# First scores of an attention and expert kernel spread over four PSUM banks, and the first k's parts built right behind the first q's

## The chip, the cores and the metric

One Trainium2 chip, one NeuronCore. The metric is the device time of one execution in microseconds (us). Engines: PE (TensorE, matmuls), DVE (VectorE), ACT (ScalarE), POOL (GpSimd), SP (SyncE, which here issues DMAs only). ACT and POOL have DMA queues of their own beside SP's.

## The reference, cut to what matters

```python
def attention(x_norm, encodings, ...):            # 16 sequences, each 128 channels x 512 tokens
    qkv = transpose(x_norm) @ w_in.T + b_in       # 8 heads of 16
    scores = einsum("bqhd,bkhd->bhqk", q, k) / 4
    scores = where(abs(q_index - k_index) <= 64, scores, lowest)
    o = softmax(scores) @ v
    y = relu(transpose(o @ w_out.T + b_out)) * encodings
    return einsum("nit,io->not", y, w_ct) + b_ct

x = x + attention(layernorm(x), ctx)
x = x + experts(layernorm(x))                     # 16 experts, top 2, and one shared expert
```

## The kernel before, in words

The work falls into three stages: the attention of 16 sequences, a drain that mixes the last sequences with the first blocks of the shared expert, and the experts. Only the very beginning of the first stage is touched by the change.

**Order of the work.** Each engine runs a list written out by hand. A global counter, the unit `U`, runs from -26 upward, and each engine's `step(U)` calls what is due. `at(U, k)` gives sequence n when `U = 8 n + k`; `piece(U, k)` gives sequence n and one of its eight pieces j when `U = 8 n + j + k`. A piece is one block of 128 queries and four of the eight heads. Engines execute their lists strictly in order and meet through semaphores. So what stands behind a waiting call on an engine waits too.

**The first q and k (n = 0).** The layer norm of a sequence is `first_moments` on DVE (L1177, L1179; due at -26), three small operations on POOL, and `normalise1` on ACT (L932; due at -21, but for sequence 1 at `SECOND_NORM`, -10). `first_moments(n)` waits for `normalise1(n-1)`. Then PE projects q (`project_q`, L630, at -13) and k (`project_k`, L638, at -9; for n = 0 directly behind). A float32 value is carried as three bfloat16 parts. For q: `first_q` (ACT L947, -12), `residue_q` (DVE L1189, -12), `second_q` (ACT L951, -11), `third_part` (POOL L439, -11). For k: `first_k` (ACT L957, -8), `residue_k` (DVE L1195, -8), `second_k` (ACT L961, -7), `third_part` (POOL, -7). The parts are copied by DMA into stacks of 96 rows, `qstack` and `kstack`, six DMAs each (groups 0 to 5; `Q_PARTS` and `K_PARTS` say which part a group holds). SP issues them with `send_q` (L316) and `send_k` (L321); two of the first k's (groups 1 and 4) are issued by ACT (L1014). Behind these on ACT stand `biases_out`, `normalise1(2)` (at -5) and `first_q(1)` (at -4), on DVE `residue_q(1)` (-4) and `first_moments(3)` (-2).

**Scores.** `scores(n, j, half)` (PE L583, due at -1) multiplies the stacks, two heads of a piece into the bank `s1[half]`, each 192 or 256 columns. `maximum(n, j, half)` (DVE L1208, due at -1) adds the mask and takes the row maxima of that bank and counts the semaphore `rowmax` up. There are two banks `s1`, so the scores of unit u + 1 in a bank wait for the maxima of unit u in it. Between the scores PE also does `project_k` of the next sequence (at -9), `project_v` (L644, at 1), `project_q` (at -13) and `turn_max` (L654, at 8).

**Second scores.** When the 16 halves of a sequence have their maxima, POOL splits the maxima into three parts (`split_max`, L456 to L462, at 7), PE transposes them (`turn_max`, which also waits for `residue_k` of sequence n + 2), DVE copies them out (`max_rows`, L1216, at 9), SP sends them into the q stack (L347, at 9), and from unit 11 on PE computes the scores again, shifted by the maxima, into the two banks `s2` (`shifted_scores`, L601). ACT takes their exponentials (L974), POOL cuts the band (L468, L470), PE multiplies with v (L618). From there on each unit carries a piece of each of these steps. The banks `s2` are empty until unit 11.

Quoted, the wait that paces the first scores:

```python
after(pe, rowmax, 2 * UNITS * n + 2 * j + half - 1)
```

Of the kernel before, what the change touches and what calls it, by code (L numbers as in the profile page):

```python
# [28 lines left out]
ALU = mybir.AluOpType  # L29
# [5 lines left out]
HEADS, D = 8, 16  # L35
# [12 lines left out]
UNITS = 2 * QB  # L48
RING = 4
WD_RING = 3  # L50
FIRST_UNIT, LAST_UNIT = -26, UNITS * (SEQS - 1) + 40
DRAIN, DRAINED, SOON = UNITS * (SEQS - 1) + 20, 8, 2
FIRST_SOON = DRAIN - 11
SECOND_NORM = -10
MASKED = -1e38

# [49 lines left out]
def xattn_moe_kernel(nc, x, ctx_in, const_f, const_b, w_small, w_gu, w_d, sw_gu, sw_d, out):  # L107
    es = ExitStack()
    with es:
# [116 lines left out]
        bank = [es.enter_context(nc.psum_tensor(f"bank{i}", [P, 512], F32)) for i in range(8)]  # L226
        s1, s2, oacc, misc = bank[0:2], bank[2:4], bank[4:6], bank[6:8]

        consts_in, bands_in, weights_in, shared_in = (  # L230
            sem(s) for s in ("consts_in", "bands_in", "weights_in", "shared_in"))
# [70 lines left out]
        def _(sp):  # L302
# [33 lines left out]
            def step(U):  # L336
# [19 lines left out]
                    store_turned(n)  # L356
                if (n := at(U, -10)) is not None:
                    send_q(n, (1, 3))
                if (n := at(U, -9)) is not None:
                    sp.wait_ge(q_p2, n + 1)  # L360
                    send_q(n, (2, 4))
                if (n := at(U, -7)) is not None:
                    sp.wait_ge(q_p3, n + 1)
                    send_q(n, (5,))
                    sp.wait_ge(k_p1, n + 1)
                    send_k(n, (0,))
                if (n := at(U, 25)) is not None:
                    after(sp, gated_ready, n - 1)
                    sp.dma_start(enc[n % 2], ctx_in[n]).then_inc(enc_in[n % 2], 16)
                if (n := at(U, -6)) is not None:  # L370
                    send_k(n, (2, 5))
                    if n > 0:
                        sp.wait_ge(k_p2, n + 1)
                        send_k(n, (1,))
                if (n := at(U, -5)) is not None:
# [45 lines left out]
        def _(pool):  # L421
# [57 lines left out]
            def step(U):  # L479
                if (n := at(U, -24)) is not None:  # L480
                    inverse_deviation(0, n, mom1, eps1, rstd1)
                    mean_shift(0, n, rstd1, shift1)
                if (n := at(U, 30)) is not None:
                    gate(n)
                if (n := at(U, 7)) is not None:
                    split_max(n)
                if (n := at(U, 23)) is not None:
                    split_reciprocals(n)
                if (n := at(U, 35)) is not None:
                    inverse_deviation(1, n, mom2, eps2, rstd2)  # L490
                    mean_shift(1, n, rstd2, shift2)
                if p := piece(U, 11):
                    cut_band(*p)
                if (n := at(U, -11)) is not None:
                    third_part(n, qres, qparts, q_p2, q_p3)
                if (n := at(U, -7)) is not None:
                    third_part(n, kres, kparts, k_p2, k_p3)

            v.memset(kstack[0][STACK:STACK + 3, :, :], -1.0).then_inc(ones_set, 1)
# [57 lines left out]
        def _(pe):  # L557
# [15 lines left out]
            def scores(n, j, half):  # L573

                blk, hg = j // 2, j % 2
                lo, w, _ = window(blk)
                if j == 0 and half == 0:
                    pe.wait_ge(q_in[n % RING], STACK_DMAS * (n // RING + 1))
                    pe.wait_ge(k_in[n % RING], STACK_DMAS * (n // RING + 1))
                after(pe, rowmax, 2 * UNITS * n + 2 * j + half - 1)  # L580
                for i in range(2):
                    h = 4 * hg + 2 * half + i
                    last = mm(s1[half][:, 256 * i:256 * i + w],  # L583
                              qstack[n % RING][0:STACK, h, P * blk:P * blk + P],
                              kstack[n % RING][0:STACK, h, lo:lo + w], start=True, stop=True)
                last.then_inc(s1_ready, 1)

            def shifted_scores(n, j, half):
# [3 lines left out]
                if j == 0 and half == 0:  # L592
# [3 lines left out]
                        pe.wait_ge(ones_in, 16 * (RING - 1))  # L596
                    pe.wait_ge(max_in[n % RING], 16 * (n // RING + 1))
                after(pe, exp_ready, 2 * UNITS * n + 2 * j + half - 1)
                for i in range(2):
                    h = 4 * hg + 2 * half + i  # L600
                    last = mm(s2[half][:, 256 * i:256 * i + w],  # L601
                              kstack[n % RING][0:STACK + 3, h, P * blk:P * blk + P],
                              qstack[n % RING][0:STACK + 3, h, lo:lo + w], start=True, stop=True)
# [308 lines left out]
        def _(act):  # L912
# [83 lines left out]
            def step(U):  # L996
# [5 lines left out]
                    first_q(n)  # L1002
                if (n := at(U, 36)) is not None:
                    normalise2(n)
                if (n := at(U, -11)) is not None:
                    second_q(n)
                if (n := at(U, -8)) is not None:
                    first_k(n)
                if (n := at(U, -7)) is not None:
                    second_k(n)  # L1010
                    if n == 0:
                        act.wait_ge(k_p2, 1)
                        for g in (1, 4):
                            act.dma_start(kstack[0][g:STACK:STACK // D, :, :],  # L1014
# [151 lines left out]
        def _(dve):  # L1166
# [31 lines left out]
            def maximum(n, j, half):  # L1198
# [5 lines left out]
                    after(dve, m_step, 4 * (n - 2) + 2)  # L1204
                dve.wait_ge(s1_ready, 2 * UNITS * n + 2 * j + half + 1)
                for i in range(2):
                    o = s1[half][:, 256 * i:256 * i + w]
                    last = v.tensor_tensor_reduce(o, o, cb[:, B_MASK + off:B_MASK + off + w], 1.0, MASKED * 2.0,  # L1208
                                                  ALU.add, ALU.max, rowmaxes[n % 2][:, h + i, blk:blk + 1])
                last.then_inc(rowmax, 1)  # L1210
# [34 lines left out]
            def step(U):  # L1245
# [7 lines left out]
                    maximum(*p, 0)  # L1253
                if (n := at(U, 40)) is not None:
                    logits_out(n)
                if (n := at(U, -8)) is not None:
                    residue_k(n)
                if (n := at(U, 34)) is not None:
                    second_moments(n)
                if (n := at(U, 27)) is not None:  # L1260
# [336 lines left out]
```

## Time and profile before

| | us |
|---|---|
| runs of the kernel before | 704.88, 708.72, 709.67 (median 708.72) |
| profiled execution, its own time | 707.8 |
| profiled execution, its span | 706.1 |
| PE busy | 650.6 (92% of the span) |
| DVE busy | 389.7 (55%) |
| ACT busy | 358.4 (51%) |
| POOL busy | 430.3 (61%) |

### The profile page before, as it was taken

Reading aid. Unit: us, or ns where it says so; the run is one execution under the profiler, and the core shown is the slowest. Engines: PE = TensorE matmul, PEld = TensorE weight load, DVE = VectorE, ACT = ScalarE, POOL = GpSimd, SP = SyncE. Lnnn points to the kernel's source line nnn. Section 1 sums busy time; section 2 is a strip of 40 time slices with the busy share of each in tenths; the row PEclk is TensorE's granted clock in tenths of the full one; section 3 lists DMA queues with packets and bytes.
Section 4 is the critical chain, followed back from the end, with each engine's and each line's share of the span. In section 5 each row is a group of like instructions: output and inputs, shape, how many; then the busy total and the mean of one; then the engine's idle time right before and its main releaser. Section 6 shows DMA issues by size and latency. Waiting matters only on the chain. (4 is left out here: it accounts for less than half of the span.)

```text
span 706.1 us, 13862 instructions
## 1 busy us (share of the span) xinstructions
PE 650.6 (92%) x4070; PEld 316.2 (45%) x4070; DVE 389.7 (55%) x1424; ACT 358.4 (51%) x673; POOL 430.3 (61%) x653
## 2 busy tenths in 40 slices
PE   3679899999999999999899999999999999999992
PEld 1345555555555555554444545333333333333330
DVE  3788888888888888771232679422222222222220
ACT  4247777777777777556511311344444354444441
POOL 5247788888888887667411001357767577768653
PEclk9569999999999999999999999999999999999997
DMA  6643545655444454332289881645655556554420
GB/s 207 159 117 95 143 131 148 169 169 152 131 127 141 136 138 139 104 94 63 64 306 408 314 330 60 207 90 106 122 125 111 149 126 121 116 97 93 81 44 0
DMA packets 67579, 99.45 MB, mean 141 GB/s; under 512 B 18601, under 2 KB 43305, under 8 KB 65449
## 3 DMA queue, kind: packets, MB, share of 16 engines
q1 hardware_dynamic: 52848, 70.68, 32.4%
q0 software_dynamic: 9600, 18.89, 14.7%
q10 hardware_dynamic: 5058, 8.99, 3.7%
q8 instruction: 35, 0.57, 0.3%
q14 instruction: 38, 0.31, 0.1%
HBM read 50.99 MB, written 23.33 MB: 105 GB/s over the span
## 5 line engine op out<-in xcount | busy, mean ns | idle before, releaser
L1208 DVE CUSTOM_DVE_ANT_0 bank<-bank,cb 128x192 f32<-128x192 f32 (+1 forms) x512 | 185.8, 416 | 35.6 <-PE bank L583 35.3
L974 ACT ACTIVATE wgu<-bank 128x384 f32<-128x384 f32 (+1 forms) x256 | 125.6, 547 | 49.5 <-PE bank L601 49.1
L806 PE MATMUL bank<-wgu,rowsT 128*64 x320 | 145.9, 599 | 0.0
L808 PE MATMUL bank<-X,rowsT 128*64 128x512 f32 x320 | 145.9, 598 | 0.0
L1452 DVE TENSOR_TENSOR act_in<-act_in,bank 128x256 f32<-128x256 f32 x56 | 23.5, 420 | 189.5 <-ACT act_in L1103 189.5
L583 PE MATMUL bank<-wgu 96*128 96x192 bf16 (+1 forms) x512 | 95.4, 272 | 20.6 <-DVE wgu L1208 14.7
L468 POOL TENSOR_SCALAR_AFFINE_SELECT wgu<-wgu 128x512 f32<-128x512 f32 (+1 forms) x128 | 74.6, 582 | 51.9 <-ACT wgu L974 51.7
L514 POOL DMA_INDIRECT rows<-xn_rows,gather_i x40 | 46.0, 1150 | 74.8 <-DVE gather_i L1438 54.5
L532 POOL DMA_INDIRECT out<-y_out,scatter x40 | 61.5, 1539 | 37.7 <-DMA out<-y_out,scatter_i 19.2
L532 POOL DMA_INDIRECT out<-y_out,scatter_i x40 | 63.1, 1577 | 31.2 <-issue 20.3
L583 PEld LDWEIGHTS bank<-wgu 96*128 96x128 bf16 x512 | 45.5, 102 | 81.5 <-issue 40.0
L837 PE MATMUL bank<-X,actT 128*64 x160 | 75.3, 593 | 2.1 <-issue 2.1
L806 PEld LDWEIGHTS bank<-wgu,rowsT 128*64 128x64 f32 x320 | 40.6, 136 | 75.2 <-issue 75.2
L470 POOL TENSOR_SCALAR_AFFINE_SELECT wgu<-wgu 128x512 f32<-128x512 f32 (+1 forms) x128 | 74.2, 580 | 0.0
L601 PE MATMUL bank<-wgu 99*128 99x192 bf16 (+1 forms) x512 | 72.1, 261 | 1.1 <-ACT wgu L974 0.9
L1208 DVE DVE_READ_ACCUMULATOR2_ANT wgu<- 128x1 f32 x512 | 71.4, 140 | 0.0
L618 PE MATMUL bank<-wgu 128*32 128x192 f32 (+1 forms) x1024 | 63.5, 364 | 2.0 <-POOL wgu L470 2.0
L1096 ACT ACTIVATE y_out<-bank,gate_of 128x512 f32<-128x512 f32 (+1 forms) x40 | 27.5, 687 | 65.9 <-PE bank L839 39.5
L1467 DVE COPY X<-wgu 128x2048 f32 x40 | 49.3, 1234 | 14.2 <-issue 13.1
L601 PEld LDWEIGHTS bank<-wgu 99*128 99x128 bf16 x512 | 45.8, 97 | 12.7 <-ACT wgu L974 5.1
L1103 ACT ACTIVATE act_in<-bank 128x256 f32<-128x256 f32 x56 | 21.5, 385 | 58.3 <-PE bank L808 44.6
L1085 ACT COPY actT<-bank 128x256 f32<-128x256 f32 x56 | 20.4, 367 | 56.6 <-PE bank L817 54.1
(176 smaller groups left out, 1085.3 us busy)
## 6 DMA issues: line engine op xcount, KB each, us to landing
wgu<-wgu SPq DMA_DIRECT2D x190, 128.0 KB, 2.7
wgu<-w_gu SPq DMA_DIRECT2D x16, 1024.0 KB, 13.1
X<-w_d SPq DMA_DIRECT2D x16, 512.0 KB, 4.1
out<-y_out ACTq DMA_DIRECT2D x17, 256.0 KB, 5.0
X<-x SPq DMA_DIRECT2D x16, 256.0 KB, 3.4
wgu<-ctx SPq DMA_DIRECT2D x16, 256.0 KB, 3.3
xn_rows<-xn SPq DMA_DIRECT2D x16, 256.0 KB, 2.4
xn_turned<-xn2T SPq DMA_DIRECT2D x16, 256.0 KB, 3.4
```

What stands on the lines that cost most here:

```text
L468: v.affine_select(out=before, in_=before, compare_op=ALU.is_ge, fill=0.0, base=off, pattern=[[0, 4], [1, P - off]], channel_multiplier=-1)
L470: v.affine_select(out=behind, in_=behind, compare_op=ALU.is_ge, fill=0.0, base=0, pattern=[[0, 4], [-1, w - P + off]], channel_multiplier= ...
L532: nc.gpsimd.indirect_dma_start(out_rows[:, :], bass.IndirectOffsetOnAxis(ap=to[0:GROUP, j:j + 1], axis=0), y_out[GROUP * g:GROUP * g + GRO ...
L583: last = mm(s1[half][:, 256 * i:256 * i + w], qstack[n % RING][0:STACK, h, P * blk:P * blk + P], kstack[n % RING][0:STACK, h, lo:lo + w], ...
L601: last = mm(s2[half][:, 256 * i:256 * i + w], kstack[n % RING][0:STACK + 3, h, P * blk:P * blk + P], qstack[n % RING][0:STACK + 3, h, lo:l ...
L618: last = mm(oacc[hg][32 * i:32 * i + 32, lo:lo + w], vaug[n % 3][:, blk, 4 * hg + i, :], probs[j % 4][:, i, 0:w], start=(blk == 0), stop=( ...
L806: mm(gb[k.buf][0:GROUP, :], rowsT[:, k.buf, c, 0:GROUP], wgu[:, bass.ds(e * 2048 + 512 * c, 512)], start=(c == 0), stop=(c == 3))
L808: last = mm(gb[k.buf][GROUP:P, :], rowsT[:, k.buf, c, GROUP:P], gu_half[:, k.buf, 512 * c:512 * c + 512], start=(c == 0), stop=(c == 3))
L837: mm(yb[k.buf][0:GROUP, :], actT[:, k.buf, c, 0:GROUP], wd[:, bass.ds(place * 1024 + 512 * c, 512)], start=(c == 0), stop=(c == 1))
L974: nc.scalar.activation(probs[j % 4][:, 2 * half:2 * half + 2, 0:w], s2[half][:].rearrange("p (j c) -> p j c", j=2)[:, :, 0:w], ACT.Exp, sc ...
L1208: last = v.tensor_tensor_reduce(o, o, cb[:, B_MASK + off:B_MASK + off + w], 1.0, MASKED * 2.0, ALU.add, ALU.max, rowmaxes[n % 2][:, h + i, ...
L1467: v.tensor_copy(gu_half[:, k.buf, :], wgu[:, bass.ds(e * 2048, 2048)]).then_inc(half_ready, 1)
```

## The change

1. In units 0 to 9 the scores of odd units go into the banks `s2`, those of even units into `s1`. The waits of `scores` follow (`held_maxima`): in units 0 to 10 a half waits for the maxima of the unit two before it. `shifted_scores(0, 0, half)` waits for the maxima of unit 9.
2. For sequence 0 the k parts are made earlier: `first_k(0)` on ACT and `residue_k(0)` on DVE move from unit -8 to -11, ahead of `second_q(0)` on ACT. The third part of k moves from POOL to DVE.
3. `normalise1(1)` on ACT moves from unit -10 to -8.
4. The stack DMAs of sequence 0: SP issues q 0, 1, 3, then k 0, 2, 5, then q 5, then k 3; ACT issues q 2, 4 and k 1, 4 behind `second_k(0)`.

```diff
+WIDE = 10
-SECOND_NORM = -10
+SECOND_NORM = -8
...
+        def scores_bank(n, j, half):
+            u = UNITS * n + j
+            return s2[half] if u < WIDE and u % 2 == 1 else s1[half]
+
+        def held_maxima(n, j, half):
+            u = UNITS * n + j
+            return 2 * u + half - (3 if u <= WIDE else 1)
...
                 if (n := at(U, -10)) is not None:
                     send_q(n, (1, 3))
-                if (n := at(U, -9)) is not None:
+                if U == -9:
+                    sp.wait_ge(k_p1, 1)
+                    send_k(0, (0, 2, 5))
+                elif (n := at(U, -9)) is not None:
                     sp.wait_ge(q_p2, n + 1)
                     send_q(n, (2, 4))
                 if (n := at(U, -7)) is not None:
                     sp.wait_ge(q_p3, n + 1)
                     send_q(n, (5,))
-                    sp.wait_ge(k_p1, n + 1)
-                    send_k(n, (0,))
+                    if n > 0:
+                        sp.wait_ge(k_p1, n + 1)
+                        send_k(n, (0,))
...
                 if (n := at(U, -6)) is not None:
-                    send_k(n, (2, 5))
                     if n > 0:
+                        send_k(n, (2, 5))
                         sp.wait_ge(k_p2, n + 1)
                         send_k(n, (1,))
...
-                if (n := at(U, -7)) is not None:
+                if (n := at(U, -7)) is not None and n > 0:
                     third_part(n, kres, kparts, k_p2, k_p3)
...
-                after(pe, rowmax, 2 * UNITS * n + 2 * j + half - 1)
+                after(pe, rowmax, held_maxima(n, j, half))
...
-                    last = mm(s1[half][:, 256 * i:256 * i + w],
+                    last = mm(scores_bank(n, j, half)[:, 256 * i:256 * i + w],
...
                 after(pe, exp_ready, 2 * UNITS * n + 2 * j + half - 1)
+                if n == 0 and j == 0:
+                    pe.wait_ge(rowmax, 2 * (WIDE - 1) + half + 1)
...
+                if U == -11:
+                    first_k(0)
                 if (n := at(U, -11)) is not None:
                     second_q(n)
-                if (n := at(U, -8)) is not None:
+                if (n := at(U, -8)) is not None and n > 0:
                     first_k(n)
                 if (n := at(U, -7)) is not None:
                     second_k(n)
                     if n == 0:
+                        act.wait_ge(q_p2, 1)
+                        for g in (2, 4):
+                            act.dma_start(qstack[0][g:STACK:STACK // D, :, :],
+                                          qparts[:, Q_PARTS[g], :]).then_inc(q_in[0], 16)
                         act.wait_ge(k_p2, 1)
...
-                    o = s1[half][:, 256 * i:256 * i + w]
+                    o = scores_bank(n, j, half)[:, 256 * i:256 * i + w]
...
-                if (n := at(U, -8)) is not None:
+                if (n := at(U, -8)) is not None and n > 0:
                     residue_k(n)
+                if U == -11:
+                    residue_k(0)
+                if U == -7:
+                    dve.wait_ge(k_res, 1)
+                    dve.wait_ge(k_p2, 1)
+                    v.tensor_tensor(kparts[:, 2, :], kres, kparts[:, 1, :], ALU.subtract).then_inc(k_p3, 1)
```

## Rows read from the trace of the kernel before

**Rows 1.** The page's first line.

```profile
span 706.1 us, 13862 instructions
```

**Rows 2.** Two stretches: us, busy by engine (instructions), PE clock, DMA share, GB/s.

```profile
19.20:37.00 17.80, 12.52 (x46) 6.12 (x47) 13.84 (x70) 4.01 (x6) 4.51 (x6) 0.60 0.63 170
...
90.00:130.00 40.00, 38.25 (x324) 22.31 (x325) 33.70 (x154) 28.06 (x55) 33.37 (x73) 1.00 0.54 145
```

**Rows 3.** DVE groups by form, 19.5 to 37.1: busy, mean ns, idle before.

```profile
L1208 DVE CUSTOM_DVE_ANT_0 bank<-bank,cb 128x256 f32<-128x256 f32 x16 | 6.4, 450 | 2.5 <-PE bank L583 2.5
L1208 DVE CUSTOM_DVE_ANT_0 bank<-bank,cb 128x192 f32<-128x192 f32 x17 | 5.6, 386 | 1.4 <-PE bank L583 1.4
```

**Rows 4.** DVE's waits, 19.5 to 45.5: us in total, times, longest.

```profile
DVE bank L1208 <- PE bank L583: 6.4, 7, 1.3
```

**Rows 5.** Timeline of unit 0: start, duration, engine, line [idle before].

```profile
19.21 0.80 PE L583 MATMUL bank<-wgu 96*128 96x192 bf16 x4 [5.79 <-DMA wgu<-wgu]
...
19.80 1.96 PE L638 MATMUL bank<-wgu 128*128 128x512 f32 x2
...
22.12 0.37 DVE L1208 CUSTOM_DVE_ANT_0 bank<-bank,cb 128x192 f32<-128x192 f32 x1 [1.03 <-PE bank L583]
```

**Rows 6.** Timeline, later units: DVE's idle stretches and PE beside them.

```profile
24.57 1.91 PE L644 MATMUL bank<-wgu 128*128 128x128 f32 x8
...
26.95 0.43 DVE L1208 CUSTOM_DVE_ANT_0 bank<-bank,cb 128x256 f32<-128x256 f32 x1 [1.26 <-PE bank L583]
...
29.04 1.91 PE L630 MATMUL bank<-wgu 128*128 128x512 f32 x2
...
31.41 0.43 DVE L1208 CUSTOM_DVE_ANT_0 bank<-bank,cb 128x256 f32<-128x256 f32 x1 [1.25 <-PE bank L583]
...
39.62 0.36 DVE L1208 CUSTOM_DVE_ANT_0 bank<-bank,cb 128x192 f32<-128x192 f32 x1 [1.34 <-PE bank L583]
...
44.44 0.43 DVE L1208 CUSTOM_DVE_ANT_0 bank<-bank,cb 128x256 f32<-128x256 f32 x1 [0.92 <-PE bank L583]
...
45.38 0.39 PE L583 MATMUL bank<-wgu 96*128 96x256 bf16 x2 [0.54 <-DVE wgu L1208]
```

**Rows 7.** Timeline of the first q and k, to the DMA issues.

```profile
9.01 1.89 PE L638 MATMUL bank<-wgu 128*128 128x512 f32 x2
...
10.08 0.75 DVE L1189 SCALAR_TENSOR_TENSOR wgu<-bank,wgu 128x512 f32<-128x512 f32 x1
...
11.43 0.81 ACT L932 ACTIVATE wgu<-X,wgu 128x512 f32<-128x512 f32 x1
...
12.15 0.67 ACT L957 ACTIVATE wgu<-bank,wgu 128x512 bf16<-128x512 f32 x1
...
12.34 0.69 DVE L1177 BATCH_NORM_STATS2 wgu<-X 128x6 f32<-128x512 f32 x1 [1.51 <-ACT wgu L932]
...
13.17 0.72 DVE L1195 SCALAR_TENSOR_TENSOR wgu<-bank,wgu 128x512 f32<-128x512 f32 x1
...
13.89 2.56 SPq L321 DMA_DIRECT2D wgu<-wgu  x4
13.92 0.62 ACT L961 CAST wgu<-wgu 128x512 bf16<-128x512 f32 x1 [1.11 <-DVE wgu L1195]
...
14.57 1.51 ACTq L1014 DMA_DIRECT2D wgu<-wgu  x2
14.62 1.15 POOL L439 TENSOR_TENSOR wgu<-wgu 128x512 bf16<-128x512 f32 x1
```

**Rows 8.** DMA issues from 15.7 (SP) and 15.0 (ACT): the last two issued of each.

```profile
L321 SPq DMA_DIRECT2D wgu<-wgu x2: 598/604/609, 15.2 to 15.8; - x2
...
DMA to landing us min/median/max: 3.1/3.2/3.3
```

**Rows 9.** Stretches again: before the first rise of the clock, and early in the full load.

```profile
14.58:31.10 16.52, 10.04 (x34) 5.39 (x35) 9.67 (x44) 5.04 (x10) 4.51 (x7) 0.50 0.70 187
...
50.00:55.00 5.00, 4.71 (x35) 2.79 (x36) 4.40 (x25) 2.93 (x6) 4.02 (x8) 0.67 0.61 159
```

## The prediction, made before the change was run

> **What bounds the kernel now.** I read the page first, then the stretches by engine, then the waits, then the timeline of the first 50 us. The page gives a span of 706.1 us [rows 1]; the profiled execution itself took 707.8, so 1.7 us lie around the span. The stretches show two regimes. From 90 to 130 us PE is busy 38.25 of 40 us at the full clock, while DVE has 33.70 and the others less: PE bounds the full load, and nothing there is touched. From 19.2 to 37 us PE is busy only 12.52 of 17.8 us and DVE 13.84 [rows 2]: this is the fill, in which only first scores and projections run and neither engine is full. The full load starts with the first shifted scores in unit 11, right behind the scores that PE starts at 45.38 [rows 6]. What has to be done behind that point is the same before and after, so the change is worth what it moves that point forward.
>
> Why is the fill slow? With two banks a half of unit u + 1 can only be computed when the same half of unit u has its maxima. When PE then does a projection of about 1.9 us, DVE has no finished scores in stock and stands idle. DVE waited for scores 7 times between 19.5 and 45.5, 6.4 us in all [rows 4]; 3.9 us of these (2.5 and 1.4) fall before 37.1 [rows 3]. Reading the timeline for what PE did: 1.03 us ended at 22.12 (behind the projection of k(1), 19.80 for 1.96) [rows 5], 1.26 at 26.95 (behind v(0), 24.57 for 1.91), 1.25 at 31.41 (behind q(2), 29.04 for 1.91), 1.34 at 39.62 (behind k(2)), 0.92 at 44.44 (behind v(1)) [rows 6]. The other two, 0.6 together, are the very first and one of 0.2 near 41.9. All but a little of the fill runs at PE's lower clock: the granted clock is 0.50 from 14.58 to 31.1 [rows 9].
>
> **Part 1: four banks.** With two units of scores in flight, DVE can have up to two units in stock. A unit of four reductions costs it 1.4 us: of the 13.84 us busy between 19.2 and 37, 2.4 are two residues and one set of moments, and 11.4 over 33 reductions are 0.35 each [rows 2, 3]. One unit in stock covers most of a projection of 1.9 us. I follow PE and DVE unit by unit.
> - Unit 1: PE's order is scores of unit 0, k(1), scores of unit 1. The wait of unit 1 never bound, k(1) did. This 1.03 stays. Saved: 0.
> - Units 1 to 3: PE goes from unit 1 straight to unit 2 (before, it waited for DVE), ends there near 23.2, does v(0) to 25.1, and has the first half of unit 3 near 25.7. DVE is through unit 2 at 25.4. The 1.26 shrink to 0.3. Saved: 1.0.
> - Unit 5, behind q(2): PE reaches q(2) at 27.2, at the low clock it ends at 29.0 and the scores come at 29.6, while DVE is through unit 4 at 28.7; at the full clock they come at 28.6. PE is nearly unbroken busy from 19 on in this version, where before it had gaps, and the clock rose at 31.1 behind two unbroken us; I take the full clock here. The 1.25 go, saved 1.25; at the low clock only 0.3 of it, which also counts on.
> - Unit 9, behind k(2): unit 8's scores are done two units early, k(2) is through at 34.4, DVE needs unit 9 at 35.7. Saved: 1.34, and the small 0.2 by the same reason, 1.5 together.
> - Unit 11, behind v(1): unit 11 waits for the unit before it again. v(1) stands behind the transposed maxima, which stand behind DVE's residue of k(2); so PE can't run ahead here, and DVE, which comes with less delay, waits 1.3 in place of 0.92. Lost: 0.4.
>
> Sum: 1.0 + 1.25 + 1.5 - 0.4 = 3.35, say 3.4 us. Bounds: with the low clock throughout, 3.4 - 0.95 = 2.4; with no wait of DVE at all but that of unit 1, the two remaining ones (0.3 and 1.3) go too, 5.0. The added wait of the first shifted scores for the maxima of unit 9 costs nothing: PE's wait for unit 11's maxima ahead of it is later. Behind the transposed maxima stand max_rows, SP's DMA and the shifted scores; before, the whole took from 41.5 to at most 45.5, and here it has from 37.9 to 41.6, as long.
>
> **Parts 2 to 4: the first q and k.** The trace shows the path of k: its projection ends at 10.90; first part 12.15 (0.67), behind the normalising of sequence 1 (11.43, 0.81); residue 13.17 (0.72), behind the moments of sequence 2 (12.34); second part 13.92 (0.62); third part on POOL 14.62 (1.15), so 15.77; then SP's last issue at 15.8 [rows 7, 8]. It landed at about 19.05 and the scores started at 19.21 [rows 5]. In the new order, with the same durations: first part of k 10.95 to 11.65; residue 11.7 to 12.45; second part of q to 12.25; normalising of sequence 1 to 13.0; second part of k to 13.6; moments of sequence 2 on DVE 13.05 to 13.95; third part on DVE to 14.65. The trace has no such subtraction on DVE. POOL's took 1.15, DVE's residue of the same size 0.72, DVE's reduction over 192 columns 0.39 [rows 3]: I take 0.7 as nearest, and the range is 0.39 to 1.15. SP has issued q 0, 1, 3 and k 0, 2, 5 by 13.8 at 0.64 each (2.56 over 4 [rows 7]), q 5 by 14.4, and k 3 at 14.75, a microsecond earlier than now.
>
> But ACT now has four issues in place of two. At 0.755 each (1.51 over 2 [rows 7]) from 13.65 the last one starts at 15.9. The last two of ACT landed 3.1 to 3.3 us behind their issue [rows 8], which gives 19.1; with the last issue lying a little further from the crowd, 18.9. So the first scores start 0 to 0.3 earlier; I take 0.2. If ACT came to its issues only at 14.57 as now, the last would land at 14.57 + 3 x 0.755 + 3.3 = 20.1, 1.1 late: the other bound.
>
> The Trainium skill bears on this: "DMA: Bandwidth & Descriptors", section "Issuing engines are not separate DMA queues", says that DMAs started by different engines run on the same 16 DMA engines, and that a second issuer saves only issue time. The longer landing of 3.1 to 3.3 us, seen while both queues were issuing, agrees with it. If the second queue were free of the first, the last would land as quickly as an early one and about 0.9 us sooner; by the rule it doesn't, and the rest of this text counts with the row.
>
> What stands behind ACT's four issues: the biases, normalising of sequence 2, first part of q(1); behind these DVE's residue of q(1) and moments of sequence 3, which stand ahead of the first maxima. They come about 0.6 us later, DVE is free at 19.9 instead of 19.3. This costs nothing, since DVE idles 1.03 us behind k(1) anyway. If that cover were gone it would cost up to 0.6. POOL's third part of q(0) comes 0.7 later, and only SP's q 5 waits for it, which is due then.
>
> **Sum.** 3.4 + 0.2 = 3.6 us, between 1.3 (2.4 with the stack 1.1 late) and 5.3. Against the profiled execution: 707.8 - 3.6 = 704.2. The median of the three timed runs lies 0.9 above that execution and the lowest 2.9 below; the four together have a mean of 707.8, so I leave 704.2 as it is.
>
> **The rivals.**
> - *The lead is larger (chance 0.2).* PE, never short of a free bank, gets the full clock early and through unit 11: then DVE alone paces the fill, 5.3 us, 702.5. If one of the low-clock stretches behind the fill goes too (50 to 55 us shows 0.67 for 5 us, 1.65 us lost [rows 9]), 700.9. For it: PE's gaps go. Against: in units 5 to 8 PE has little to do at the full clock and may be throttled again. The Trainium skill has the mechanism in "TensorE: Matmul & The Clock Gate", section "A second HAM failure mode: psum-queue depth-cycling": small idles of PE between groups that cycle through PSUM banks make the clock swing, and the rises and falls are paid each time. This trace shows such swings.
> - *The stack comes late (0.15).* ACT reaches its four issues later, or the twelve transfers slow each other, and the first scores start 1 us later. 707.8 - 3.4 + 1.1 = 705.5.
> - *The change doesn't do what it says (0.1).* PE's order of projections, not the banks, sets the pace, or the lead is waited out again at unit 11, because the DMA of the maxima or the transfers of sequence 2 hold it. For it: the 1.03 at unit 1 is of this kind. Time as before, 707.8.
> - *Slower (0.05).* The denser first units put PE's quiet units 5 to 8 so that the clock is low when the full load begins, and further such stretches follow. There PE bounds, and each stretch costs 1.65 us [rows 9]. It takes a third one beyond those of before to eat the 3.6: 707.8 - 3.6 + 4.95 = 709.2. Against: the full load itself keeps PE dense.
>
> **How the numbers follow.** The forecast as summed has 0.5, 704.2, with a range of its own of 702.7 to 705.7. The single runs spread over 4.8 us, so a median wanders by one or two. The range over the cases is 700.8 to 708.3: below it lie part of the first rival, above it part of the last two. A measurement of this kernel tells about 1% (7 us) from no change. Faster by more than 1%, below 701.6 seen from the median, takes the larger lead and luck with the clock, 0.14; slower by more than 1% needs five low stretches, 0.03; within 1%, 0.83.
>
> **What would show it.** In the changed profile the scores of unit 12 and the first shifted scores (L601 there) should start near 41.7 in place of 45.5; DVE's idle ahead of maxima should be 1 us at unit 1, then near none until 1.3 us at unit 11; the sixteenth half of sequence 0 should be through near 34.4 in place of 36.9; first scores at 19.0; the DVE subtraction near 14.0 for 0.7 us; and the stretches of 40 us behind 90 should look as before. It is wrong if the first shifted scores move by less than 2.4 or more than 5.3, or if they move and the end does not.

## The result, and the profile after

The changed kernel took 701.87 us (median of 10 runs, 700.51 to 704.92), the kernel before 705.96 in the same number of runs (704.05 to 709.67). The ratio is 0.9951, with a 95% interval of 0.9933 to 0.9970: 4.1 us between the medians, 2.1 to 4.7 us by the interval. Timed once more on another occasion the ratio was 0.9929 (0.9903 to 0.9955). So the change makes the kernel faster by about half a per cent. The profiled execution of the changed kernel took 701.98 us with a span of 700.2.

"Fill" below is the time from PE's first scores to its first shifted scores (before: 19.21 to 45.60, 26.4 us; changed: 18.91 to 41.58, 22.7 us). The fill, in the timeline of the changed kernel (start, duration, engine, line; the scores are now L596, k is L653, v L659, q L645, the shifted scores L616, the maxima L1229). These lines answer to [rows 5] and [rows 6]:

```profile
18.91 0.80 PE L596 MATMUL bank<-wgu 96*128 96x192 bf16 x4 [5.11 <-DMA wgu<-wgu]
...
19.51 1.96 PE L653 MATMUL bank<-wgu 128*128 128x512 f32 x2
...
21.83 0.37 DVE L1229 CUSTOM_DVE_ANT_0 bank<-bank,cb 128x192 f32<-128x192 f32 x1 [0.43 <-PE bank L596]
...
22.76 1.68 PE L659 MATMUL bank<-wgu 128*128 128x128 f32 x8
...
26.66 1.10 PE L645 MATMUL bank<-wgu 128*128 128x512 f32 x2 [0.86 <-issue]
...
33.10 1.97 PE L653 MATMUL bank<-wgu 128*128 128x512 f32 x2
...
35.42 0.37 DVE L1229 CUSTOM_DVE_ANT_0 bank<-bank,cb 128x192 f32<-128x192 f32 x1 [0.32 <-PE bank L596]
...
40.25 0.43 DVE L1229 CUSTOM_DVE_ANT_0 bank<-bank,cb 128x256 f32<-128x256 f32 x1 [0.92 <-PE bank L596]
...
41.18 0.61 PE L596 MATMUL bank<-wgu 96*128 96x256 bf16 x2 [0.54 <-DVE wgu L1229]
...
41.58 0.85 PE L616 MATMUL bank<-wgu 99*128 99x192 bf16 x4
```

Look at the brackets of the DVE lines, which give DVE's idle time just before. The idle of 1.26 behind v(0) and of 1.25 behind q(2) have no line any more: DVE never stands still there in this execution. That behind k(2) went from 1.34 to 0.32. That behind v(1), in front of unit 11, is 0.92 as before, and so is the small 0.20 ahead of unit 10. The waits of DVE from 19 to 41.5 sum this up, beside 6.4 us of before [rows 4]:

```profile
DVE bank L1229 <- PE bank L596: 1.9, 4, 0.9
```

The scores of unit 12 start at 41.18 in place of 45.38, 4.2 us earlier. DVE, in the stretch of [rows 2], is busy 16.98 of 17.8 us in place of 13.84; it has become the pace of the fill:

```profile
19.20:37.00 17.80, 12.29 (x55) 7.12 (x53) 16.98 (x87) 5.51 (x9) 6.48 (x13) 0.69 0.63 174
```

PE has a new wait of its own in the fill, ahead of unit 8, the first unit of sequence 1. Its scores in the changed kernel, and in a later execution of it ("changed, timed" in the table further down):

```profile
32.50 0.80 PE L596 MATMUL bank<-wgu 96*128 96x192 bf16 x4 [1.55 <-DVE wgu L1229]
```

```profile
32.73 0.80 PE L596 MATMUL bank<-wgu 96*128 96x192 bf16 x4 [1.79 <-DMA wgu<-wgu]
```

The first names DVE, but DVE was through unit 6, for whose maxima unit 8 waits, by 31.8, and a transfer into the k stack of sequence 1 was issued at 26.6 and landed at 32.4:

```profile
L330 SPq DMA_DIRECT2D wgu<-wgu x1: 596/596/596, 26.6 to 26.6; - x1
DMA to landing us min/median/max: 5.8/5.8/5.8
```

So PE, far ahead, is held there by the stack of sequence 1, and k(2) and the scores of unit 9 come behind.

The path of the first k, which answers to [rows 7]:

```profile
10.71 0.69 ACT L972 ACTIVATE wgu<-bank,wgu 128x512 bf16<-128x512 f32 x1 [0.88 <-PE bank L653]
...
11.81 0.81 ACT L947 ACTIVATE wgu<-X,wgu 128x512 f32<-128x512 f32 x1
...
12.23 0.70 ACTq L1031 DMA_DIRECT2D wgu<-wgu  x1
12.53 0.60 ACT L976 CAST wgu<-wgu 128x512 bf16<-128x512 f32 x1
...
13.55 0.67 DVE L1284 TENSOR_TENSOR wgu<-wgu 128x512 bf16<-128x512 f32 x1
13.61 1.27 ACTq L1035 DMA_DIRECT2D wgu<-wgu  x2
...
13.88 0.63 SPq L325 DMA_DIRECT2D wgu<-wgu  x1
...
14.55 0.66 SPq L330 DMA_DIRECT2D wgu<-wgu  x1
...
17.85 0.69 ACT L962 ACTIVATE wgu<-bank,wgu 128x512 bf16<-128x512 f32 x1 [1.69 <-DMA wgu<-wgu]
```

Everything is issued by 15.2, where before SP's last issue started at 15.8 [rows 8]. Yet the scores start only 0.3 us earlier here. (Over all profiles it is 0.7: with the issues of before they start at 19.21, 19.72 and 19.45, with the new ones at 18.59 to 18.91 in eight executions, 18.76 on average.) The query of SP's last issue (k 3, at 14.55) shows how long it took to land, and beside it stand the stretches from 15 to 18 us of the changed kernel and of the kernel before (columns as in [rows 2]):

```profile
DMA to landing us min/median/max: 4.2/4.2/4.2
```

```profile
15.00:18.00 3.00, 0.00 (x0) 0.00 (x0) 0.00 (x0) 1.21 (x4) 0.26 (x1) 0.50 1.05 226
```

```profile
15.00:18.00 3.00, 0.00 (x0) 0.00 (x0) 0.23 (x1) 1.61 (x4) 0.77 (x1) 0.50 0.92 263
```

In the changed kernel the busy share of the DMA engines is 1.05, that is full, and no PE or DVE work runs. The last transfer was issued 1.2 us earlier and took 1 us longer to land. The 226 GB/s are not a ceiling: the kernel before moved 263 in this stretch at a share of 0.92. Why the transfers occupied the engines longer is not shown.

### The profile page after: what moved, and what is told of

Same layout as the page of the kernel before. It is cut to its first block and busy times, and to the rows that moved or that the text cites. A ratio compares the mean times of both kernels' runs of the same rounds, so it can differ in the third digit from the quotient of the medians.

```text
span 700.2 us, 13863 instructions
## 1 busy us (share of the span) xinstructions
PE 647.5 (92%) x4070; PEld 316.8 (45%) x4070; DVE 389.8 (56%) x1425; ACT 358.4 (51%) x673; POOL 427.8 (61%) x652
## 5 line engine op out<-in xcount | busy, mean ns | idle before, releaser
L1229 DVE CUSTOM_DVE_ANT_0 bank<-bank,cb 128x192 f32<-128x192 f32 (+1 forms) x512 | 185.8, 418 | 30.9 <-PE bank L596 30.7
L1479 DVE TENSOR_TENSOR act_in<-act_in,bank 128x256 f32<-128x256 f32 x56 | 23.6, 421 | 189.4 <-ACT act_in L1124 189.4
L596 PE MATMUL bank<-wgu 96*128 96x192 bf16 (+1 forms) x512 | 93.8, 270 | 18.0 <-DVE wgu L1229 12.7
L596 PEld LDWEIGHTS bank<-wgu 96*128 96x128 bf16 x512 | 46.1, 102 | 75.0 <-issue 38.4
L616 PE MATMUL bank<-wgu 99*128 99x192 bf16 (+1 forms) x512 | 72.8, 262 | 1.1 <-ACT wgu L989 0.9
L1229 DVE DVE_READ_ACCUMULATOR2_ANT wgu<- 128x1 f32 x512 | 72.9, 142 | 0.0
L616 PEld LDWEIGHTS bank<-wgu 99*128 99x128 bf16 x512 | 46.1, 98 | 13.2 <-ACT wgu L989 5.3
```

Source lines behind the costliest of these rows:

```text
L596: last = mm(scores_bank(n, j, half)[:, 256 * i:256 * i + w], qstack[n % RING][0:STACK, h, P * blk:P * blk + P], kstack[n % RING][0:STACK, ...
L616: last = mm(s2[half][:, 256 * i:256 * i + w], kstack[n % RING][0:STACK + 3, h, P * blk:P * blk + P], qstack[n % RING][0:STACK + 3, h, lo:l ...
```

## The experiments

The change has two halves, so the first two kernels take one each; beside them both kernels of the case ran once more for a second profile.

**Banks alone** (the kernel before, plus only this and the two functions `scores_bank` and `held_maxima` of the change):

```diff
+WIDE = 10
...
-                after(pe, rowmax, 2 * UNITS * n + 2 * j + half - 1)
+                after(pe, rowmax, held_maxima(n, j, half))
...
-                    last = mm(s1[half][:, 256 * i:256 * i + w],
+                    last = mm(scores_bank(n, j, half)[:, 256 * i:256 * i + w],
...
+                if n == 0 and j == 0:
+                    pe.wait_ge(rowmax, 2 * (WIDE - 1) + half + 1)
...
-                    o = s1[half][:, 256 * i:256 * i + w]
+                    o = scores_bank(n, j, half)[:, 256 * i:256 * i + w]
```

> Only the four banks for units 0 to 9 are added to the kernel before; the first k and the stack DMAs stay. Theory (the banks carry the lead): first scores at 19.2 as before, idle of DVE between the first maxima and unit 11 from 6.4 down to about 2 us, the scores of unit 12 near 41.4 in place of 45.4, time 3.5 to 4 us under before. Rival (the earlier k and the moved normalising carry a good part): unit 12 not before 43, time less than 2.5 us under before.

Measured: 702.72 us beside 706.68, ratio 0.9957 (0.9934 to 0.9979), the whole effect of the change within what the runs can tell. The first scores and the first shifted scores in its timeline, and DVE's waits from 19 to 41:

```profile
19.45 0.80 PE L592 MATMUL bank<-wgu 96*128 96x192 bf16 x4 [5.48 <-DMA wgu<-wgu]
...
40.55 0.49 PE L612 MATMUL bank<-wgu 99*128 99x192 bf16 x4 [0.20 <-issue]
```

```profile
DVE bank L1219 <- PE bank L592: 1.3, 2, 1.0
```

The fill took 21.1 us, before 26.4. That is even shorter than in the changed kernel (22.7), for two reasons that the trace shows. PE had the full clock from 35.2 on, through unit 11: v(1) took 1.06 in place of 1.92, and the idle of 0.92 is gone. And the stack of sequence 1 was there at 31.95, in place of 32.50, so that DVE did not wait ahead of unit 9 though k(2) ran at the low clock (1.97).

**The early k alone** (the changed kernel with two banks):

```diff
-WIDE = 10
+WIDE = 0
...
-            return 2 * u + half - (3 if u <= WIDE else 1)
+            return 2 * u + half - 1
...
-                if n == 0 and j == 0:
-                    pe.wait_ge(rowmax, 2 * (WIDE - 1) + half + 1)
```

> The changed kernel with two banks for the first scores again; the early first k, the moved normalising and the two-queue stack DMAs stay. Theory: first scores at 18.9, unit 12 near 45.1, that is 0.3 earlier than before, time 0 to 0.5 us under before, not measurable. Rival: unit 12 by 44 or earlier and time 1.5 us or more under before.

Measured: 705.85 beside 706.68, ratio 1.0001 (0.9977 to 1.0024). Timeline, then DVE's waits from 19 to 45:

```profile
18.70 0.80 PE L596 MATMUL bank<-wgu 96*128 96x192 bf16 x4 [4.88 <-DMA wgu<-wgu]
...
45.12 0.49 PE L614 MATMUL bank<-wgu 99*128 99x192 bf16 x4
```

```profile
DVE bank L1227 <- PE bank L596: 5.2, 6, 1.3
```

All of the idle but that at unit 1 is back, and the fill takes 26.4 us as before. The first scores start 0.5 us before those of the first profile (0.7 by the averages above), and the whole time shows nothing of it; its interval leaves room for up to 1.6 us. The second queue has no share in the 0.7, as the experiment with it below shows; which of the other early parts makes it was not separated.

**Both kernels once more.**

> The kernel before once more, for a second profile of it. Theory (the two profiles differ by 5.9 us in span and only 4.2 at unit 12, because the low-clock stretches behind the fill fall differently from execution to execution): the fill up to unit 12 is the same as in the first profile within 0.3 us, but the low-clock stretches behind 50 us (51.6, 290.5 and 311 in the first) fall elsewhere or are other in number, each worth about 1.6 us. Rival (they belong to the kernel before): the same three at the same places.

> The changed kernel once more, for a second profile of it. Theory: unit 12 at 41.2 within 0.3 us, low-clock stretches behind 50 us at other places or other in number than in its first profile (51.3 and 65 there). Rival: the same ones, and none behind 290 us, which would make these 3 us a part of the gain.

The kernel before: first scores at 19.72, first shifted at 46.31, the same seven idles of DVE (1.03, 1.26, 1.26, 1.34, 0.20, 0.93, and 0.18 at the first), 710.37 us. The changed kernel: 18.59, 40.83, idles 0.23, 0.20, 0.92, and 699.81 us. The fill as such takes the same from execution to execution within 0.5 us, but where it lies moves more than the 0.3 that I had expected, by 0.3 to 0.8. The low-clock stretches of the kernel before fell elsewhere (near 53, 70 and 292 us). Those of the changed kernel lay where they had been, with none behind 290, so for that run the rival held; only the third execution of this kernel, with one at 288, broke it. They are the subject of a section of their own below.

**The second queue** (q 2 and 4 back on SP):

```diff
                     sp.wait_ge(k_p1, 1)
                     send_k(0, (0, 2, 5))
+                    sp.wait_ge(q_p2, 1)
+                    send_q(0, (2, 4))
...
-                        act.wait_ge(q_p2, 1)
-                        for g in (2, 4):
-                            act.dma_start(...)
```

> The changed kernel, but q 2 and 4 of sequence 0 go through SP's queue again (behind k 0, 2, 5), so ACT issues only k 1 and 4. Theory (twelve transfers lie on the same 16 DMA engines, and either queue ends about the same time): SP has two more issues of 0.65 us, its last at about 15.9 to 16, first scores 0.3 to 0.9 us later than in the changed kernel (19.0 to 19.6). Rival (the second queue is worth its full issue time and more): later than 19.9; other rival: not later at all.

Measured: SP's last issue is at 15.71, 1.2 us later than in the changed kernel, and it lands 2.9 us behind its issue in place of 4.2:

```profile
18.76 0.80 PE L598 MATMUL bank<-wgu 96*128 96x192 bf16 x4 [4.12 <-DMA wgu<-wgu]
```

The first scores start at 18.76, within the 18.59 to 18.91 of the changed kernel. Not later at all: the other rival held. What limits here is the transfers and not their issue, as far as one execution can say. One thing does become later: ACT's first part of q(1) waits for the last q transfer and starts at 18.39 in place of 17.85, which DVE's idle at unit 1 covers. The fill took 22.9 us, with DVE idle for 0.58 ahead of unit 5: PE's clock fell at 26.9, and q(2) took 1.82.

**How far the lead carries** (four banks in units 0 to 3 only):

```diff
-WIDE = 10
+WIDE = 4
```

> The changed kernel, but only units 0 to 3 use four banks. Theory (each covered projection counts by itself): the idle ahead of unit 3 (1.26, behind v(0)) is covered, those ahead of units 5 and 9 (1.25 and 1.34) are back, first shifted scores at 43.4 to 44.0. Rival (the lead, once won, carries over the later projections): at 42.5 or earlier.

Measured: first scores at 18.65, first shifted at 42.23. The fill takes 23.6 us, 2.8 less than before, where all ten units give 3.7. Its idle stretches of DVE:

```profile
21.57 0.36 DVE L1229 CUSTOM_DVE_ANT_0 bank<-bank,cb 128x192 f32<-128x192 f32 x1 [0.43 <-PE bank L596]
...
36.25 0.36 DVE L1229 CUSTOM_DVE_ANT_0 bank<-bank,cb 128x192 f32<-128x192 f32 x1 [1.34 <-PE bank L596]
38.51 0.43 DVE L1229 CUSTOM_DVE_ANT_0 bank<-bank,cb 128x256 f32<-128x256 f32 x1 [0.20 <-PE bank L596]
41.07 0.43 DVE L1229 CUSTOM_DVE_ANT_0 bank<-bank,cb 128x256 f32<-128x256 f32 x1 [0.93 <-PE bank L596]
```

The time is the rival's (42.5 or earlier), and each theory has half of the mechanism. The idle behind k(2) is back, 1.34 to the hundredth. The one behind q(2) is not: q(2) starts at 26.41 and takes 1.10 us at the full clock, while DVE still has unit 4 to do. So this projection is covered if PE reaches it ahead of DVE and at the full clock; the stock of four banks is needed once more only at unit 9.

**PE's clock in the fill** (five unused projections in PE's idle time ahead of unit 0, then three):

```diff
+                if (n := at(U, -1)) == 0:
+                    for _ in range(5):
+                        mm(s2[0][:], wsm[:, W_Q:W_Q + P], xn1[0], start=True, stop=True)
```

> The changed kernel with five extra float32 projections of 512 columns, whose results nobody uses, on PE ahead of the scores of unit 0, where PE otherwise idles for 5 us; they are written to a bank s2 that unit 1 overwrites. Theory (what is left of the fill behind the banks is PE at the low clock): the clock is at its full level at the first scores, k(1) takes 1.0 us in place of 1.96, unit 12's scores start 0.5 to 1.5 us earlier than in the changed kernel (39.7 to 40.7), time 0.5 to 1.5 us under it. Rival (DVE alone paces the fill now): unit 12 within 0.2 us of 41, time as the changed kernel. Other rival: the extra work delays the first scores.

> The changed kernel with three unused projections ahead of unit 0 in place of five, so that they end before the stack has landed. Theory: first scores near 18.8 as in the changed kernel, at the full clock, k(1) in 1.0 us; DVE then starts unit 1 right behind unit 0 (0.3 to 0.5 us won), and the fill ends 0.3 to 1.0 us earlier than in the changed kernel (40.8 to 41.6). Rival: DVE alone paces the fill, and unit 12 moves by less than 0.3.

The five ran into the time of the first scores, in this timeline:

```profile
19.76 0.50 PE L596 MATMUL bank<-wgu 96*128 96x192 bf16 x4
20.09 1.05 PE L653 MATMUL bank<-wgu 128*128 128x512 f32 x2
```

The scores start 0.9 us late, and then k(1) takes 1.05 in place of 1.96. But the clock fell at 26.3, q(2) took 2.04, and DVE stood idle for 0.92 ahead of unit 5. First shifted scores at 41.72, nothing won; ratio 0.994 (0.991 to 0.997). With three the scores start at 18.98, PE keeps the full clock until 31.9, and the first shifted scores come at 40.30, a fill of 21.3 us, 1.4 shorter than that of 22.7 and more than I had expected at most. But a part of that is luck: in this execution the clock was full from 35.4 to 45.6, as in that of the banks alone, so that there was no idle ahead of unit 11. The whole time is 702.47, ratio 0.9944 (0.9918 to 0.9969), beside 0.9929 for the changed kernel on the same chip: no gain that can be measured.

**Unit 10 ahead of the transposed maxima**, alone, with the warming, and alone again beside the changed kernel:

```diff
-                if p := piece(U, -1):
+                if (p := piece(U, -1)) and U != 9:
                     scores(*p, 0)
...
-                if p := piece(U, -1):
+                if (p := piece(U, -1)) and U != 9:
                     scores(*p, 1)
+                if U == 8:
+                    scores(1, 2, 0)
+                    scores(1, 2, 1)
```

> The changed kernel with the scores of unit 10 computed by PE ahead of the first transposed maxima, where PE waits 1.2 us for DVE's residue of k(2), and not behind them. Theory (unit 11's idle of 0.92 comes from v(1) standing behind both): the idle of DVE ahead of unit 11 falls to 0.3 or less, unit 12 starts 0.6 us earlier (40.3 to 40.7), time 0 to 1 us under the changed kernel. Rival (the transposed maxima themselves set unit 11): unit 12 unchanged.

> Both of the two edits: the five unused projections ahead of unit 0 and unit 10's scores ahead of the transposed maxima. Theory: they add up, unit 12 at 39.3 to 40.1, time 1 to 2.5 us under the changed kernel, 5 to 6.5 under before. Rival: DVE is the pace already with one of them, and unit 12 comes no earlier than with the better of the two.

> The kernel with unit 10's scores ahead of the transposed maxima once more, beside the changed kernel on one chip. Theory (DVE's idle ahead of unit 11 is gone, 0.6 to 1.2 us): first shifted scores 0.5 to 1.5 us earlier than in the changed kernel, median 0.3 to 2 us under it. Rival: the gain is in the granted clock of single executions only, and the medians agree within 0.3 us.

> The changed kernel, timed on the same chip as the kernel with unit 10 ahead. Theory: 3 to 5 us under before, as first measured.

In the first profile DVE has no idle at all from 19 to 40, and the fill takes 21.2 us (18.68 to 39.86); from 24 to 41 us DVE is busy 16.96 of 17:

```profile
24.00:41.00 17.00, 11.44 (x62) 6.54 (x61) 16.96 (x90) 5.96 (x10) 5.10 (x10) 0.87 0.56 156
```

That does not yet credit the edit: PE had the full clock there from 35.1 to 45.4 and v(1) took 1.11, and with the full clock the idle ahead of unit 11 was gone without the edit too (banks alone, three projections). The test is the second profile, where PE had the low clock from 33.6 to 43.8 and v(1) took 2.02. The projection q(2), and DVE ahead of units 5 and 11:

```profile
26.68 1.95 PE L645 MATMUL bank<-wgu 128*128 128x512 f32 x2 [0.95 <-issue]
...
29.10 0.43 DVE L1232 CUSTOM_DVE_ANT_0 bank<-bank,cb 128x256 f32<-128x256 f32 x1 [0.76 <-PE bank L596]
...
39.87 0.43 DVE L1232 CUSTOM_DVE_ANT_0 bank<-bank,cb 128x256 f32<-128x256 f32 x1 [0.47 <-PE bank L596]
```

At the low clock the idle ahead of unit 11 falls from 0.92 to 0.47, and to 0.27 in the version with the warming (v(1) 1.86). So half of it or more comes from v(1) standing behind the transposed maxima. The fill takes 22.35 us, because 0.76 of idle is back ahead of unit 5: the clock had fallen at 26.8, just as q(2) began. The whole time: 0.9917 (0.9884 to 0.9951) the first time, 0.9949 (0.9924 to 0.9974) the second, beside 0.9929 (0.9903 to 0.9955) for the changed kernel on the chip of the second; the median is 702.31 beside 701.56, so the gain of 0.3 to 2 us that I had expected did not come. With the warming 0.9907 (0.9871 to 0.9943), though in its profile the first scores come at 20.18 and nothing is won at unit 12 (first shifted 41.63). A few tenths of a microsecond in the fill are in the profiles; a version that is faster than the changed kernel was not shown.

## What the clock gives and takes behind the fill

The two profiled executions that I first compared differ by 5.9 us in span, but only by 4.2 at the scores of unit 12. SP's issues mark the same work in both. The last load of x, and the first load of the experts' weights, in the kernel before:

```profile
222.01 0.60 SPq L304 DMA_DIRECT2D X<-x  x1
356.55 0.43 SPq L334 DMA_DIRECT2D wgu<-w_gu  x1
```

and in the changed kernel:

```profile
219.25 0.59 SPq L313 DMA_DIRECT2D X<-x  x1
350.66 0.93 SPq L343 DMA_DIRECT2D wgu<-w_gu  x2
```

The lead is 2.8 us at 220 us and 5.9 at 350. Between them lies only this difference (before, then changed; the clock is the third column from the end):

```profile
290.00:320.00 30.00, 27.84 (x235) 16.62 (x239) 19.77 (x101) 17.51 (x35) 18.13 (x39) 0.89 0.29 87
```

```profile
290.00:320.00 30.00, 28.23 (x259) 16.91 (x257) 20.14 (x96) 18.37 (x36) 22.59 (x50) 1.00 0.25 70
```

All fourteen profiled executions, read the same way. "Stretches" are the short low-clock stretches between 280 and 315 us (in the second profile of the kernel before the two follow each other without a gap, 292 to 299 us):

| kernel | fill, us | first shifted | shifted to the x load near 65 to 73 | last x load to weights | stretches there |
|---|---|---|---|---|---|
| before | 26.4 | 45.60 | 25.4 | 134.5 | 2 |
| before, again | 26.6 | 46.31 | 26.7 | 134.5 | 2 |
| early k alone | 26.4 | 45.12 | 24.1 | 133.0 | 1 |
| four banks in units 0 to 3 | 23.6 | 42.23 | 25.4 | 134.4 | 2 |
| changed | 22.7 | 41.58 | 26.5 | 131.4 | 0 |
| changed, again | 22.2 | 40.83 | 26.7 | 131.5 | 0 |
| changed, timed | 22.9 | 41.80 | 25.5 | 133.3 | 1 |
| banks alone | 21.1 | 40.55 | 25.1 | 131.6 | 0 |
| unit 10 ahead, again | 22.4 | 41.20 | 26.4 | 131.5 | 0 |
| unit 10 ahead | 21.2 | 39.86 | 25.1 | 133.0 | 1 |
| second queue | 22.9 | 41.66 | 25.3 | 131.3 | 0 |
| five projections | 22.0 | 41.72 | 25.5 | 133.2 | 1 |
| three projections | 21.3 | 40.30 | 25.1 | 131.6 | 0 |
| five, and unit 10 ahead | 21.5 | 41.63 | 26.7 | 132.8 | 1 |

The fifth column follows the sixth: 131.3 to 131.6 us with none, 132.8 to 133.3 with one, 134.4 or 134.5 with two, so about 1.5 us for each stretch. Their number differs between executions of one and the same kernel (0, 0, 1 for the changed one), so the 3.1 us that the first pair of profiles shows there can't be counted as a lasting part of the gain. The executions with two banks had 2, 2 and 1, that with four banks in units 0 to 3 had 2, and the ten with ten wide units had 4 in all. Whether the change makes such stretches rarer stays open with so few; the 4.1 us between the medians need no such help, since the fill alone is 3.7 us shorter and starts a little earlier.

The fourth column shows where a part of the lead goes. In the kernel before the clock rises to its full level at 44.9, just ahead of the full load; the changed kernel reaches the full load at 41.6, and PE, which bounds there, has the low clock until 44.5. The way from the first shifted scores to the x load takes 26.5 to 26.7 us in two of its executions and 25.5 in the third, against 25.4 and 26.7 before and 24.1 where no low stretch fell into it. So in the first pair about 1 us of the lead of 4 is given back, by where the clock happens to stand; the averages of these few (26.2 us changed, 26.0 before) show no lasting loss. From that x load to the last one the first nine rows take 151.0 to 151.4 us, the other five 151.4 to 152.7, the most where another low stretch fell wholly into it, near 75 us (unit 10 ahead, the second queue).

## Why the prediction was right, and where its steps were off

Forecast 704.2 us, a gain of 3.6; measured 701.87 and 4.1 by the medians. The direction, the place and the size of the gain held, and so did its split between the two halves of the change. Within the four banks the size held partly by luck, because errors of opposite sign cancelled: forecast 1.0 + 1.25 + 1.5 - 0.4 = 3.35 us, in the first profile of the changed kernel 1.26 + 1.25 + 1.02 + 0 = 3.53. The absolute time is 2.3 us lower than forecast: I started from the profiled execution of 707.8, and the median of ten runs of the kernel before was 705.96. That is 1.8 of the 2.3. And an interval of 2.1 to 4.7 us can't tell 3.6 from 4.1.

- *The banks, 3.4 us.* Shown by the first two experiments: banks alone 0.9957, all but the banks 1.0001. The fill became 3.7 us shorter.
- *Units 1 to 3, 1.26 shrinking to 0.3.* It shrank to nothing, and not by the clock: it was nothing too where v(0) took the full 1.91 us of the low clock (in the names of the table: changed, timed; unit 10 ahead; four banks in units 0 to 3). PE was simply earlier than I had counted: it began v(0) at 22.76 and not near 23.2, and DVE had unit 2 until 25.2.
- *Unit 5 at the full clock.* Right in this execution: q(2) took 1.10, and before the rise at 24.1 PE had worked without a gap from 18.9. Before, with gaps, it rose at 31.2. But this was in part luck. Of the eleven profiled executions with four banks, seven had the full clock through q(2) and no idle ahead of unit 5; in four it fell at 26.3 to 27.9, q(2) took 1.71 to 2.04, and 0.58 to 0.94 of the idle stayed. That is the price which I had set at 0.95 for the low clock.
- *Unit 9 fully covered.* Not fully: 0.32 of the 1.34 stay, and all of the small 0.20, which I had counted with it. I had PE free to run two units ahead and k(2) through at 34.4; it was through at 35.07. What I had left out is the stack of sequence 1: PE's scores of unit 8 waited for it until 32.50, and k(2) stands behind them, at the low clock (1.97), since the clock had fallen at 30.9 after PE had done little from 28 on. With unit 8's scores at 32.73 and 32.35 the idle was 0.56 and 0.57 (changed, timed; three projections, which had DVE 0.4 us ahead), at 31.76 to 31.95 there was none (changed, again; unit 10 ahead; banks alone).
- *Unit 11, the idle growing from 0.92 to 1.3.* Wrong: with v(1) at the low clock and unit 10 in its old place it was 0.92 or 0.93 in every execution, with two banks or four. v(1) stands behind the transposed maxima, these behind DVE's residue of k(2), and DVE's next work hangs on both: the whole knot moves with DVE and doesn't change. I had let PE's side lag by 0.4 that don't exist. Putting unit 10 ahead takes half or more of the 0.92, the full clock all of it.
- *The first unit.* I had kept the 1.03 in full. It was 0.43, because DVE came 0.33 later to the first maxima (20.06, forecast 19.9) and k(1) ended 0.3 earlier. The same in the sum, since PE paces there.
- *The first q and k.* Starting time right (18.91 for 19.0, though the step forward was 0.7 by the averages, and I had 0.2), reason off. I had ACT's four issues last until 16.7 and the last transfer land 3.1 to 3.3 behind its issue. All issues were through by 15.2, and the last to land, SP's, came 4.2 behind its own. I had DVE come late to the first maxima because ACT's issues stand ahead of the normalising of sequence 2 and of first_q(1). ACT was free for the normalising a microsecond earlier than before (15.35, before 16.33); what made first_q(1) late (17.85, before 17.05) is its wait for the q transfers, whose source it overwrites. The Trainium skill, "DMA: Bandwidth & Descriptors", section "Issuing engines are not separate DMA queues", gives the right rule: the issuing engine saves issue time alone. The trace agrees with it: 4.2 us to land, against 2.9 with two of ACT's issues back on SP, at the same start of the scores. Here issue time wasn't the limit. The DVE subtraction took 0.67, for the 0.7 taken.
- *A low-clock stretch costs 1.65.* About 1.5 by the table.

Of the rivals, "the stack comes late" and "the change doesn't do what it says" fall with the timeline. "The lead is larger", with the full clock through unit 11, came true in the profiles of three variants (banks alone, three projections, and one of unit 10 ahead), whose fills took 21.1 to 21.3 us: there DVE paces nearly all of the fill. None of these variants was shown to be faster than the changed kernel by its median. "Slower" has this much in it that low stretches can take back part of the lead; its price never reached the gain.

## What to carry to other kernels

An engine that paces a stage can be short of work only because its partner has just two buffers, and buffers that a later stage owns may stand empty in the fill: lending them there covers each long instruction in between. Read the gain from the idle stretches in the brackets of the timeline, one by one, and ask of each which engine's order, and not only which buffer, stands in front of it. When one wait is gone, look for what the engine that now runs ahead meets next: here PE met the stack of sequence 1. And an earlier issue of transfers is worth little while the transfer engines are full: two issues moved by 1.2 us did not move the start.

And compare two profiles segment by segment with markers of the same work before you credit a change with the difference of their spans: here 3.1 of the 5.9 us came from where the clock stood.

## What the runs showed of the hardware

- A DMA issue on ACT's queue does not wait for the compute that stands ahead of it on ACT to run, only for that compute's own semaphore wait. L1031 was issued at 12.23 while L947 ran (11.81 to 12.62), and L976, which stands ahead of the issue in ACT's list, started at 12.53. L976 waits for the residue of k, which DVE ended at 12.19 (11.44 for 0.75), and the issue followed by 0.04; it did so again in the second profile (11.93, 11.97) and the third (12.20, 12.24). The second part of q, for which the issue itself waits, was through at 11.91. I had counted it behind L976, at 13.65.
- Twelve transfers of 128 KB within the same SBUF, issued within 5.4 us, fill the DMA engines at the end: share 1.05 at 226 GB/s from 15 to 18 us (0.92 at 263 in the kernel before). Landing takes 4.2 us for SP's last one, 2.9 where two of ACT's go to SP and the issuing ends 1.2 us later, and 3.1 to 3.3 for ACT's two in the kernel before [rows 8]. One for the stack of sequence 1 took 5.8.
- PE's clock fell to 1.2 GHz in the changed kernel's fill (30.9) after PE had been busy for only 1.4 us of the 3 since 28. With three unused projections ahead of the first scores it was full from these to 31.9.
- Where the clock changes differs between executions of one kernel with the same work: with unit 10 ahead it was full from 24.9 to 31.7 in one profile, and from 23.4 to 26.8 and 30.2 to 33.6 in the other.
